# A two-layer graph network on one core: the weighted pass sums each block in PSUM, and GpSimd gathers in runs of sixteen

## The reference, cut to what matters

```python
# src, dst: 206250 edges sorted by dst; x: [6250, 256], normalised row by row
messages = edge_val[:, None] * embeddings[edge_src]
neighbor_emb = segment_sum(messages, edge_dst, num_segments=6250)
interaction_emb = neighbor_emb * embeddings
side_emb = (neighbor_emb + interaction_emb) @ W2.T + b2
```

## Time and profile before

| what | value |
|---|---|
| runs | 8905.07, 8915.07, 8921.09 us; median 8915.07 us |
| profiled execution, its own time | 8919.81 us |
| span of that execution | 8918.1 us |
| mean granted TensorE clock | 0.766 of full speed |
| busy: PE, PEld, DVE, ACT, POOL | 64%, 54%, 44%, 18%, 61% |

### The profile page before, as it was taken

How to read it: one execution, slowest core, us unless ns; L and a number is a source line. 1 busy time by engine, 2 the same in 40 slices (tenths; PEclk the granted TensorE clock), 3 DMA queues, 4 the chain that set the end, 5 groups by cost and what they waited for, 6 DMA issues and landing times. The chain is left out here.

```text
span 8918.1 us, 116140 instructions
## 1 busy us (share of the span) xinstructions
PE 5734.9 (64%) x27644; PEld 4860.0 (54%) x27645; DVE 3949.3 (44%) x10109; ACT 1567.7 (18%) x3440; POOL 5455.9 (61%) x5690
## 2 busy tenths in 40 slices
PE   3777777777773488881455444444446489999893
PEld 2555565555552377771333333333335488888883
DVE  4566666777777400004444434333435422222225
ACT  1122222221220233330000000000001233333331
POOL 3666666666665566665666666666666566666662
PEclk7778878888885699995777767677667677777876
DMA  3333333333333144443333322222221122222335
GB/s 111 90 88 90 89 89 88 89 88 89 88 88 109 58 147 142 143 145 113 89 89 89 87 80 80 80 80 80 80 80 42 32 70 65 65 65 65 65 65 166
DMA packets 426058, 793.32 MB, mean 89 GB/s; under 512 B 129162, under 2 KB 267134, under 8 KB 425684
## 3 DMA queue, kind: packets, MB, share of 16 engines
q0 software_dynamic: 235504, 474.87, 21.7%
q1 hardware_dynamic: 190436, 317.20, 10.6%
HBM read 720.67 MB, written 70.98 MB: 89 GB/s over the span
## 5 line engine op out<-in xcount | busy, mean ns | idle before, releaser
L1153 PE MATMUL g_pM<-g_G,g_S 128*128 x3328 | 1211.8, 542 | 1536.1 <-ACTq L1047 1072.1
L833 POOL DMA_INDIRECT g_G<-table,X x1664 | 1583.0, 951 | 922.4 <-issue 451.7
L843 POOL DMA_INDIRECT g_G<-table,g_IDX x1616 | 1539.9, 953 | 867.7 <-issue 509.9
L1153 PEld LDWEIGHTS g_pM<-g_G,g_S 128*128 128x128 f32 x3328 | 927.7, 286 | 1820.2 <-issue 1618.6
L1121 PE MATMUL g_pM<-g_G,g_S 128*128 128x260 f32 x3328 | 1257.7, 538 | 688.6 <-DVE acc L950 666.9
L1696 POOL DMA_INDIRECT q_G<-table,slot x1072 | 1040.9, 971 | 625.7 <-issue 288.3
L1121 PEld LDWEIGHTS g_pM<-g_G,g_S 128*128 128x128 f32 x3328 | 819.4, 264 | 982.2 <-DVE acc L950 748.8
L618 POOL DMA_INDIRECT slots<-sort_PAIR,sort_ADDR x1024 | 1023.3, 999 | 452.0 <-issue 294.4
L958 DVE TENSOR_TENSOR acc<-g_pM,acc 128x256 f32 x1664 | 697.8, 419 | 1351.4 <-PE g_pM L1153 623.8
L950 DVE TENSOR_TENSOR acc<-g_pM,acc 128x260 f32 x1664 | 712.5, 428 | 271.9 <-PE g_pM L1121 79.6
L938 DVE TENSOR_SCALAR g_S<-iota,g_REL,g_WT 128x128 f32<-128x128 f32 x1664 | 595.2, 358 | 193.1 <-issue 171.7
(11 more groups left out here) (334 smaller groups left out, 6881.9 us busy)
## 6 DMA issues: line engine op xcount, KB each, us to landing
e_W<-in_L_ffn_W SPq DMA_DIRECT2D x210, 512.0 KB
sort_PAIR<-slot_rows SPq DMA_DIRECT2D x66, 512.0 KB
g_G<-table,X POOLq DMA_INDIRECT x1664
g_G<-table,g_IDX POOLq DMA_INDIRECT x1616
ys_all<-ew_Y SPq DMA_DIRECT2D x196, 128.0 KB
sm_Y<-ys_all SPq DMA_DIRECT2D x28, 896.0 KB, 10.8
q_ST<-slot_rows SPq DMA_DIRECT2D x34, 512.0 KB
sort_ADDR<-slot_rows SPq DMA_DIRECT2D x34, 512.0 KB
```

The lines of the kernel that those rows point to most:

```text
L833: pool.indirect_dma_start(G[:, r, u, :], None, table, bass.IndirectOffsetOnAxis(ap=IDX[:, k * GRP + u:k * GRP + u + 1].bitcast(U32), axis= ...
L843: pool.indirect_dma_start(G[:, r, u, :], None, table, bass.IndirectOffsetOnAxis(ap=IDX[:, g * GRP + u:g * GRP + u + 1].bitcast(U32), axis= ...
L1153: m = pe.matmul(pM[r % 2 * 2 + half][:, u % HG, :], S[:, r, u, :], rows.rearrange("p a d -> p (a d)"), start=True, stop=True)
```

## The change

`graph_pass` is split into `attention_pass` (the same work as before with the branches of the other pass taken out) and `weighted_pass`, which is new.

- GpSimd gathers in 101 runs of sixteen tiles (`RUN`, `RUNS`). It waits once behind each run until both of the run's groups have landed and raises `runs`. From the third run on it loads one register, waits for `sum`, raises `room` and waits for it before it writes places of `G` again. The scatters of the sort are issued two per run ahead of the gathers, in the last 65 runs.
- SP loads, for every slot, which run it needs, waits for that run and raises `ready`; once per step it also loads and waits for a count of cleared banks.
- TensorE waits for `ready` before every slot, loads two sets of eight registers per step (place and bank), and accumulates into one of eight PSUM banks chosen by the block.
- ScalarE clears the eight banks at the start; when a block is complete it copies its bank to `acc` and clears the bank again (49 copies in all).
- VectorE builds only one-hots, eight in a row per step; its 1664 adds are gone.
- The tables are built by other operations of similar number, with six loads in place of four, and the planning stage stores one more small array.

```diff
             sp.dma_start(planned_block, BI[0:1, :]).then_inc(s["stored"], 16)
-            sp.wait_ge(s["stored"], 16 * (NA + 1))
+            sp.dma_start(planned_start, STARTI[:, :]).then_inc(s["stored"], 16)
+            sp.wait_ge(s["stored"], 16 * (NA + 2))
...
+            then(v.tensor_copy(STARTI[:, :], START[:, :]))
...
+RUN = 2 * GRP
+RUNS = NTE // RUN
+BANKS8 = 8
+
 class TileTables:
...
-    PLACE, LANDED, ROOM = 32, 64, 96
+    BLOCK_AT = 512
...
+    def banks(self, k):
+        return self.TAB[0:1, bass.ds(k * GRP, GRP)]
 
     def places(self, k):
         return self.TAB[self.PLACE:self.PLACE + 1, bass.ds(k * GRP, GRP)]
 
-    def landed(self, k, j):
-        return self.TAB[self.LANDED:self.LANDED + 1, bass.ds(k * RINGS + j, 1)]
-
-    def summed(self, g):
-        return self.TAB[self.ROOM:self.ROOM + 1, bass.ds(g, 1)]
+    def needed(self, slot):
+        return self.TAB[self.NEEDED:self.NEEDED + 1, bass.ds(slot, 1)]
+
+    def room(self, j):
+        return self.TAB[self.ROOM:self.ROOM + 1, bass.ds(j, 1)]
+
+    def cleared(self, k):
+        return self.TAB[self.ROOM:self.ROOM + 1, bass.ds(self.BLOCK_AT + k, 1)]
+
+    def complete(self, b):
+        return self.TAB[self.ROOM:self.ROOM + 1, bass.ds(b + NTE, 1)]
...
+        room = self.TAB[self.ROOM:self.ROOM + 1, :]
+        for row in (0, self.PLACE, self.NEEDED):
             sp.dma_start(self.TAB[row:row + 1, :], block).then_inc(self.s["loaded"], 16)
-        sp.dma_start(self.TAB[self.ROOM:self.ROOM + 1, 0:NTE], first).then_inc(self.s["loaded"], 16)
+        sp.dma_start(room[:, 0:RUNS - 1], first[:, RUN:NTE:RUN], allow_slow_non_contiguous=True).then_inc(self.s["loaded"], 16)
+        sp.dma_start(room[:, self.BLOCK_AT:self.BLOCK_AT + SG], block[:, GRP - 1:NS:GRP], allow_slow_non_contiguous=True).then_inc(self.s["loaded"], 16)
+        sp.dma_start(room[:, NTE:NTE + NB - 1], start.rearrange("p a -> a p")[:, 1:NB]).then_inc(self.s["loaded"], 16)
...
+        then(v.tensor_scalar(self.TAB[0:1, :], self.TAB[0:1, :], BANKS8 - 1, None, ALU.bitwise_and))
...
+        at = slice(self.NEEDED, self.NEEDED + 1)
+        need = self.TAB[at, :]
+        then(v.scalar_tensor_tensor(need, need, -1.0, self.ROW[at, :], ALU.mult, ALU.add))
+        then(v.tensor_scalar(need, need, 4, None, ALU.logical_shift_right))
+        then(v.tensor_scalar(need, need, 1.0, None, ALU.add))
...
+        n = RUNS - 1
+        room, TF = self.TAB[at, 0:n], self.TF[at, 0:n]
+        then(v.tensor_scalar(room, room, 7, None, ALU.logical_shift_right))
+        then(v.tensor_copy(TF, room))
+        then(v.scalar_tensor_tensor(room, TF, 1.0, self.ROW[at, RUN - 1:NTE - RUN:RUN], ALU.add, ALU.add))
+        blk = self.TAB[at, self.BLOCK_AT:self.BLOCK_AT + SG]
+        then(v.tensor_scalar(blk, blk, 1.0, None, ALU.add))
...
+def weighted_pass(sh, tag, planned, table, acc, acc_zeroed, gather_done, rounds0, src_tiles, tables, sort, place, tail):
+    nc = sh.nc
+    RND = SG // RINGS
+    s = {n: sh.sem(f"{tag}_{n}") for n in ("loaded", "onehot", "sum", "runs", "ready", "room", "cleared", "copied")}
+    with Scope(nc) as sc:
+        IDX = sc.sb(f"{tag}_IDX", [P, NTE], I32)
+        REL = sc.sb(f"{tag}_REL", [P, NS])
+        WT = sc.sb(f"{tag}_WT", [P, NS])
+        G = sc.sb(f"{tag}_G", [P, RINGS * GRP, D])
+        S = sc.sb(f"{tag}_S", [P, RINGS, GRP, P])
+        pB = sc.ps(f"{tag}_pB", [P, BANKS8, 512])
+        block = sc.block()
+        n_loads = 3 * 16
+        def over_groups(eng, step):
+            for r in range(RINGS):
+                step(0, r)
+            with eng.Fori(1, RND) as it:
+                for r in range(RINGS):
+                    step(it, r)
+        @block.sync
+        def _(sp):
+            sp.dma_start(IDX[:, :], src_tiles).then_inc(s["loaded"], 16)
+            sp.dma_start(REL[:, :], planned[1]).then_inc(s["loaded"], 16)
+            sp.dma_start(WT[:, :], planned[2]).then_inc(s["loaded"], 16)
+            def ready(k):
+                cleared = sp.value_load(tables.cleared(k), min_val=1, max_val=NB)
+                sp.wait_ge(s["cleared"], cleared)
+                for u in range(GRP):
+                    run = sp.value_load(tables.needed(k * GRP + u), min_val=1, max_val=RUNS)
+                    sp.wait_ge(s["runs"], run)
+                    sp.sem_inc(s["ready"], 1)
+            with sp.Fori(0, SG) as k:
+                ready(k)
+        @block.gpsimd
+        def _(pool):
+            pool.wait_ge(s["loaded"], n_loads)
+            for j in range(RUNS):
+                if j >= 2:
+                    slots = pool.value_load(tables.room(j - 2), min_val=1, max_val=NS)
+                    pool.wait_ge(s["sum"], slots)
+                    pool.sem_inc(s["room"], 1)
+                    pool.wait_ge(s["room"], j - 1)
+                if 2 * j >= TG - place:
+                    sort.place(pool, 2)
+                for n in range(RUN):
+                    t = j * RUN + n
+                    pool.indirect_dma_start(G[:, t % (RINGS * GRP), :], None, table, bass.IndirectOffsetOnAxis(
+                        ap=IDX[:, t:t + 1].bitcast(U32), axis=0)).then_inc(gather_done[t // GRP % RINGS], 16)
+                for g in (2 * j, 2 * j + 1):
+                    pool.wait_ge(gather_done[g % RINGS], (g // RINGS + rounds0 + 1) * 16 * GRP)
+                pool.sem_inc(s["runs"], 1)
+            sort.place(pool, tail)
+        @block.vector
+        def _(v):
+            v.wait_ge(s["loaded"], n_loads)
+            def onehots(rnd, r):
                 k = rnd * RINGS + r
+                at_least(v, s["sum"], (k - RINGS + 1) * GRP)
+                for u in range(GRP):
+                    j = k * GRP + u
+                    v.tensor_scalar(S[:, r, u, :], sh.iota[:, :], REL[:, bass.ds(j, 1)], WT[:, bass.ds(j, 1)],
+                                    ALU.is_equal, ALU.mult).then_inc(s["onehot"], 1)
+            over_groups(v, onehots)
+        @block.scalar
+        def _(a):
+            a.wait_ge(*acc_zeroed)
+            zero = acc[:, NB - 1, :]
+            def clear(bank):
+                a.activation(pB[:, bass.ds(bank, 1), 0:D].rearrange("p a d -> p (a d)"), zero, ACT.Copy).then_inc(s["cleared"], 1)
+            def take(b, bank):
+                a.activation(acc[:, bass.ds(b, 1), :].rearrange("p a d -> p (a d)"),
+                             pB[:, bass.ds(bank, 1), 0:D].rearrange("p a d -> p (a d)"), ACT.Copy).then_inc(s["copied"], 1)
+            for bank in range(BANKS8):
+                clear(bank)
+            def emptied(b, bank):
+                slots = a.value_load(tables.complete(b), min_val=1, max_val=NS)
+                a.wait_ge(s["sum"], slots)
+                take(b, bank)
+            with a.Fori(0, NB // BANKS8 - 1) as it:
+                for bank in range(BANKS8):
+                    emptied(it * BANKS8 + bank, bank)
+                    a.wait_ge(s["copied"], it * BANKS8 + bank + 1)
+                    clear(bank)
+            for b in range(NB // BANKS8 * BANKS8 - BANKS8, NB):
+                if b < NB - 1:
+                    emptied(b, b % BANKS8)
+                else:
+                    a.wait_ge(s["sum"], NS)
+                    take(b, b % BANKS8)
+                if b + BANKS8 < NB:
+                    a.wait_ge(s["copied"], b + 1)
+                    clear(b % BANKS8)
+            a.wait_ge(s["copied"], NB)
+        @block.tensor
+        def _(pe):
+            at_regs = [pe.alloc_register(f"{tag}_at{u}") for u in range(GRP)]
+            bank_regs = [pe.alloc_register(f"{tag}_bank{u}") for u in range(GRP)]
+            def loaded(regs, row, low, high):
+                pe.reg_load(regs, row)
+                return [pe.snap(x, min_val=low, max_val=high) for x in regs]
+            def step(rnd, r):
+                k = rnd * RINGS + r
+                at = loaded(at_regs, tables.places(k), 0, RINGS * GRP - 1)
+                bank = loaded(bank_regs, tables.banks(k), 0, BANKS8 - 1)
                 pe.wait_ge(s["onehot"], (k + 1) * GRP)
+                for u in range(GRP):
+                    pe.wait_ge(s["ready"], k * GRP + u + 1)
+                    rows = G[:, bass.ds(at[u], 1), :].rearrange("p a d -> p (a d)")
+                    sums = pB[:, bass.ds(bank[u], 1), 0:D].rearrange("p a d -> p (a d)")
+                    pe.matmul(sums, S[:, r, u, :], rows, start=False, stop=False, skip_group_check=True).then_inc(s["sum"], 1)
             pe.wait_ge(s["loaded"], n_loads)
+            over_groups(pe, step)
```

More of the change, by code:

```diff
@@ L703, in graph_pass @@
     nc = sh.nc
-    attend = keep is not None
-    ranking = attend and sort is not None
     RND = SG // RINGS
@@ L708, in graph_pass @@
     BANKS = 4
[L709 to L715, removed]
+    names = ["loaded", "onehot", "added", "iota", "part", "copied", "z", "lr", "arg", "p", "pcol", "gp",
+             "prep", "rank0", "dist", "eq", "scan", "scan_seen", "rank", "prefix", "base", "addr"]
@@ L732, in graph_pass @@
```

(32 more changed lines are left out.)

238 lines of the change are left out of this document (79 added, 159 removed).

## The result

The changed kernel takes **9492.9 us** (median of 4 runs, 9471.1 to 9495.9), the kernel before on the same chip 8911.8: ratio **1.0646** (95% interval 1.0633 to 1.0659). Slower by 6.5%, where 1.1% faster was forecast. All of it lies in the weighted pass, which takes 3155 us in place of 2582.

The account below looks back on a forecast made before the run. GpSimd's queue was taken to bound the weighted pass. Landing waits saved 181 us, less 74 handshake, 8 one-hots, 2 last stretch, 1 tables: 96 us less, 8819 us, range 8783 to 8866.

Parts of the forecast that it names:

- What moves to other queues: SP and TensorE beside GpSimd's run: 13.8 and 15.9 us fit within 22.6, so they cost nothing.
- the forecast stage: Weighted pass after the change: some 2485 us long, with GpSimd idle about 740 us before gathers.
- Rival B: SP or TensorE becomes the bound: at 1.4 us per slot, 293 us slower, 9112 us; chance 5%.
- The removed waits: GpSimd's landing waits: 101 of 202 go, 1.80 us each, 181 us saved.
- gathers at 0.95 us: GpSimd in the weighted pass: 1616 gathers still take 0.95 us each.
- bursts of one-hots: VectorE's eight one-hots in a row slow gathers by 0.04 us per burst, 8 us in all.
- rival A: VectorE's one-hot bursts shut GpSimd out of its gathers: 470 us slower, 9289 us; chance 6%.
- no adds on VectorE: VectorE loses 1664 adds, 698 us, worth nothing because VectorE waits for GpSimd.
- TensorE's step: TensorE's eight slots take at most 6.53 us, 0.82 per slot.
- handshake: GpSimd's register load, `sum` wait and `room` raise and wait: 0.75 us, 99 times, 74 us; bounds 0.44 to 1.25.
- 2.06 were taken: GpSimd's landing wait after sixteen gathers: 2.06 us, bounds 2.00 and 2.58.

Follow-up runs that it names:

- announcements by step: Changed kernel with SP loading, waiting and announcing once per eight slots, and GpSimd reporting each eight gathers after four more, without landing pauses: 0.9971 to the kernel before.
- the kernel with the pause put back: Changed kernel plus a second landing wait on GpSimd in the middle of each run, after the first eight gathers: 1.0169 to the kernel before.
- the kernel by step with one pause: Changed kernel announcing once per eight slots, plus one landing wait per run, after the first eight gathers for all of these: 0.9995 to the kernel before.
- by step with two pauses: Changed kernel announcing once per eight slots, plus a landing wait after four of each eight gathers, for these four: 1.0026 to the kernel before.
- short loop: Changed kernel with SP's loop cut to one slot an iteration and the cleared-bank wait moved to VectorE: 1.0851 to the kernel before.

## Why the prediction was wrong

- **The failed step** is "What moves to other queues": SP at "0.63 + 0.08 per slot", "13.8 us" a run, "some 6 us to spare, so they cost nothing". Both prices came from one quiet moment. In the run shown a slot took 2.9 us while GpSimd gathered and 0.83 after it, and a run of the stage needed 31.2 us in the mean, against 24.6 (the forecast stage, 2485 us, over 101 runs). At 101 us for each microsecond of lost cover that is 670 us; the whole miss is 674. Rival B named place and chain, but put 1.4 us on a slot and 5% on the case.
- **The removed waits** were the second error, hidden behind the first. 101 x 1.80 was priced as GpSimd's loss alone. In the kernel before, taking half of them away cost 0.6% and taking all away returned 0.0%; with announcements by step all of them together returned 0.55% (1.0026 to 0.9971, 49 us of 368). Other waits took their place each time; which queue made them isn't resolved for every kernel.
- **Right** were: gathers at 0.95 us (0.98 beside bursts of one-hots; rival A stayed away), no adds on VectorE, and TensorE's step (6.39 us). In the changed kernel a longer wait lies over landing and handshake, but in the kernel with the pause put back 77 of 91 run ends between 4250 and 6700 us have a wait of 3.1 to 3.4 us, so that GpSimd's own terms can be read (first fence below). The landing wait in the middle is 2.03 us (2.06 were taken); the wait at the end, with the handshake, is 3.24. That leaves 1.2 us for the handshake in place of 0.75, at the dear end of its bounds. A run without scatters lasts 24.8 us there. In the kernel by step with one pause the landing wait was 2.56 (second fence). Where the handshake doesn't stand behind a landing wait it cost nothing: by step with two pauses, the idle before 128 scatters, half of them right behind it, is 39.0 us, 0.30 each.
- That VectorE's 698 us of adds are worth nothing agrees with the kernel by step with the old pauses: without the adds, and with other changes beside, it took 1.0026.

```profile
4703.94 0.94 POOL L1123 DMA_INDIRECT g_G<-table,g_IDX  x1 [3.18 <-POOLq L1117]
...
4715.77 0.94 POOL L1123 DMA_INDIRECT g_G<-table,g_IDX  x1 [2.03 <-DMA g_G<-table,g_IDX]
...
4728.70 0.94 POOL L1123 DMA_INDIRECT g_G<-table,g_IDX  x1 [3.24 <-POOLq L1117]
```

```profile
5502.50 0.95 POOL L1126 DMA_INDIRECT g_G<-table,g_IDX  x1 [2.56 <-DMA g_G<-table,g_IDX]
```

## What to carry to other kernels

Price a queue of register loads, waits and announcements from its busiest stretch, by the minimum, median and maximum of the whole stage, and count its instructions per unit of the bounding engine's work. Before a wait on the bounding engine is booked as loss, look what the other queues do in it: here 101 more pauses made a kernel 4% faster. Announce as coarsely as the buffers allow.

## What the runs showed of the hardware

While GpSimd issued indirect DMAs back to back, one each 1.25 us, instructions that wait for nothing on SP's, ScalarE's and TensorE's queues took 0.7 or 1.4 us in place of 0.02 to 0.3. In the changed kernel SP's held records begin 2.8 us after the gathers resume, and the last one starts 2.2 us after the end of the last gather (medians). Halving the gathers' bytes or rows or a short loop did not change that, and with idle instructions on ScalarE's queue SP and ScalarE were mostly released together, on a beat of about 0.7 us. What holds them is open. Fetching of instructions by DMA does not show: over the whole execution of the changed kernel and of that with the short loop that queue moved (packets, MB, share)

```profile
q14 instruction: 87, 0.70, 0.0%
```

```profile
q14 instruction: 85, 0.70, 0.0%
```

The Trainium skill (Runtime: NRT & Kernel Launch, section Instruction fetch mechanics) says that code is fetched ahead in blocks of 16 KiB and that the fetch stays hidden, except where a taken branch leaves what is held. The packets here are of some 8 KB (0.70 MB in 87), half such a block, and a stall that comes back every 0.7 or 1.4 us, whatever the loop, is not what it describes. The Trainium skill (NOTIFIC — the notification-queue block, section Overflow: three behaviours, one of which stalls the engine) has the block that writes the trace's records hold engines back when its own pipeline is full. No run here shows whether that is at work: every execution timed here was also traced.
